# The products with V of a pair of heads in one run of four key tiles, in a differential attention and mixture-of-experts kernel

## The reference

```
Q, K: [8 batches, 16 heads, 512, 128]      V: [8, 16, 512, 64]
Q1, Q2 = Q[..., :64], Q[..., 64:]          K1, K2 likewise
A1 = Q1 @ K1.T / 8                         A2 = Q2 @ K2.T / 8
P = softmax(A1) - lam * softmax(A2)        [.., 512 queries, 512 keys]
O = P @ V                                  the products that the change moves
Y = concat_heads(O) @ Wo + bo, then a layer norm, times 0.2
```

## Time and profile before

| | before |
|---|---|
| median of 3 runs | 2054.06 us (2049.75 to 2055.78) |
| the profiled execution, its own time | 2053.49 us |
| its span in the trace | 2051.5 us |
| PE busy, share of the span | 93% |
| DVE, ACT, POOL busy | 78%, 73%, 44% |
| mean granted TensorE clock | 0.98 of full speed |

### The profile page before, as it was taken

One profiled execution on the slowest core, in us unless ns is written; L12 is line 12 of the kernel. 1 busy time (PEld: TensorE's weight loads), 2 busy tenths in 40 slices (PEclk: granted clock), 3 DMA queues, 4 the chain that ended last, 5 costly groups with the idle time before them and its releaser, 6 DMA issues. The chain is left out here.

```text
span 2051.5 us, 39312 instructions
## 1 busy us (share of the span) xinstructions
PE 1903.1 (93%) x10625; PEld 1465.2 (71%) x10625; DVE 1609.2 (78%) x2960; ACT 1493.6 (73%) x3383; POOL 909.5 (44%) x893
## 2 busy tenths in 40 slices
PE   4369999999999999999999999999998699997885
PEld 4347767776777677767767776777675699997885
DVE  5448888888888888888888888888887456664566
ACT  3348888888888888888888888888887466665332
POOL 1234444444444444444444444444433365564676
PEclk9999999999999999999999999999999899999888
DMA  5778888788778777887888787777873866672564
GB/s 174 275 226 215 210 210 215 197 210 213 209 200 212 211 206 204 212 215 198 208 211 215 198 209 212 216 195 209 211 191 78 317 222 235 244 223 98 169 213 125
DMA packets 162207, 421.05 MB, mean 205 GB/s; under 512 B 27794, under 2 KB 69568, under 8 KB 146944
## 3 DMA queue, kind: packets, MB, share of 16 engines
q1 hardware_dynamic: 157408, 410.42, 70.7%
q0 software_dynamic: 4768, 10.25, 1.8%
HBM read 177.53 MB, written 41.72 MB: 107 GB/s over the span
## 5 line engine op out<-in xcount | busy, mean ns | idle before, releaser
L567 POOL TENSOR_TENSOR e<-e,rrec 128x512 f32<-128x512 f32 x512 | 532.1, 1039 | 832.1 <-DVE rrec L683 832.1
L644 ACT ACTIVATE e<-p_score,nmax 128x512 f32<-128x512 f32 x1024 | 695.2, 684 | 136.3 <-DVE nmax L708 135.5
L708 DVE TENSOR_REDUCE nmax<-p_score 128x2 f32<-128x1024 f32 x512 | 626.8, 1224 | 152.8 <-PE p_score L766 148.4
L766 PE MATMUL p_score<-ks,qs 128*128 128x512 f32 x2048 | 575.0, 402 | 6.6 <-ACT e L644 3.8
L754 PE MATMUL p_proj<-xp,w 128*128 (+1 forms) x1920 | 524.6, 409 | 21.2 <-SPq L482 21.2
L766 PEld LDWEIGHTS p_score<-ks,qs 128*128 128x128 f32 x2048 | 369.6, 188 | 180.6 <-ACT e L644 53.9
L754 PEld LDWEIGHTS p_proj<-xp,w 128*128 128x128 f32 x1920 | 339.8, 190 | 80.4 <-SPq L482 21.9
L694 DVE SCALAR_TENSOR_TENSOR pm<-e,coef 128x512 f32<-128x512 f32 x512 | 388.9, 760 | 0.0
L611 ACT COPY pT<-p_tr 128x512 f32<-128x512 f32 x512 | 301.3, 588 | 98.4 <-PE p_tr L776 97.8
L776 PE MATMUL p_tr<-consts,pm 128*128 128x128 f32 x2048 | 307.2, 273 | 2.3 <-ACT pT L611 2.3
L776 PEld LDWEIGHTS p_tr<-consts,pm 128*128 128x128 f32 x2048 | 254.6, 140 | 71.2 <-issue 2.5
(11 more groups left out here) (137 smaller groups left out, 1735.1 us busy)
## 6 DMA issues: line engine op xcount, KB each, us to landing
ks<-k_parts SPq DMA_DIRECT2D x512, 256.0 KB, 4.3
w<-weight_parts_scratch SPq DMA_DIRECT2D x64, 1280.0 KB, 8.1
qs<-q_parts SPq DMA_DIRECT2D x512, 128.0 KB, 2.9
w<-in_w SPq DMA_DIRECT2D x46, 1024.0 KB, 7.7
oT_scratch<-oT SPq DMA_DIRECT2D x64, 256.0 KB, 4.7
oTs<-oT_scratch SPq DMA_DIRECT2D x16, 1024.0 KB, 16.5
ys_scratch<-y SPq DMA_DIRECT2D x23, 256.0 KB
weight_parts_scratch<-n_wt_parts SPq DMA_DIRECT2D x4, 1280.0 KB, 7.3
```

The source lines that it names most:

```text
L567: nc.gpsimd.tensor_tensor(e1, e1, rrec[:, t % 4, 0:1].to_broadcast([P, S]), ALU.mult).then_inc(s_e1, 1)
L644: nc.scalar.activation(ex[:, t % 4, m, :], p_score[t % 2][:, m, :], ACT.Exp, bias=nmax[:, t % 2, m:m + 1], accum_out=rsum[:, t % 4, m:m + ...
L708: nc.vector.tensor_reduce(nmax[:, t % 2, :], p_score[t % 2][:, :, :], AXX, ALU.max, negate=True).then_inc(s_max, 1)
L766: last_op = nc.tensor.matmul(p_score[st % 2][:, m, :], qs[j][u][:, m, qt * P:(qt + 1) * P], ks[j][u][:, m, part, :], start=(part == 0), st ...
```

## The change

The table that says in which step which key tiles are multiplied has one entry in place of three. The two matmuls of each key tile, their operands, their order among themselves and the waits ahead of the first of them (`s_pT`, `s_v`, `s_o`) stay as they are.

```
@@ -459,7 +459,7 @@
         ORDER = ("q0", "k0", "q1", "k1", "v", "vt")
         AT_STEP = {0: "q0", 1: "k0", 2: "q1", 3: "k1", 4: "v", 6: "vt"}
 
-        PV_STEP = {5: (0,), 6: (1,), 7: (2, 3)}
+        PV_STEP = {5: (0, 1, 2, 3)}
 
         def batch_of(pair):
             return pair // PAIRS
```

## The result

| | before | changed |
|---|---|---|
| median | 2054.31 us (4 runs) | 2068.48 us (2067.58 to 2070.21, 4 runs) |
| ratio to before | | 1.0074, 95% interval 1.0056 to 1.0091 |
| the profiled execution, its own time | 2053.49 us | 2067.92 us |
| its span | 2051.5 us | 2066.0 us |

A forecast was written before the change was run, and what follows sets the result against it. The prediction took PE to set the pace, with the other engines following. It summed 2053.5 + 11.2 (62 pairs at 0.18) + 1.5 (last pair and tail) = 2066.2, put at 2066 us; 2055 to 2079 held 8 in 10.

The forecast's parts named there:

- The wait in step 0: PE waits 0.54 us before the next pair's step 0 scores for step 6's exponentials; pair 0.18 us longer; chance 0.69.
- The entries: Two entries into the products vanish per pair, at 0.17 to 0.20 us each; 0.36 us saved.
- the rival without a wait: Step 0's scores find their buffer free at 8.72 us, so the saving stands: 2031 us, chance 0.07.
- The case without a difference: PE's wait before step 0's scores takes 0.36 us and eats just the saving: 2053 to 2058 us, chance 0.12.
- The copy of V: DVE's copy before projection k0 in step 1 keeps 0.27 us margin; rival: it becomes a second wait, 2079 us, chance 0.10.
- No debt into the next pair: From step 2 PE is slowest again; by the next step 5 all engines are back at their earlier distance.
- The clock: Expected to stay at 1.00 through the attention; rival: PE's wait lowers it, near 2230 us, chance 0.02.
- The sum: Pairs 1 to 62 add 62 x 0.18 = 11.2 us, last pair and tail 1.5 us, stages behind untouched: 2066.2 us.

The follow-up runs named there:

- short maxima: Row maxima taken over 128 of the 512 keys: in the changed kernel 2044.10 us (0.9950), in the kernel before 2049.74 us (0.9977).
- doubled transposes: Three of the four transposes of step 7 done twice: in the kernel before 2074.65 us (1.0108), in the changed kernel 2068.60 us (1.0074).
- run in step 6: All four key tiles multiplied in step 6 in place of step 5, all else as in the changed kernel: 2065.49 us, ratio 1.0047.

## Why the prediction was right

**The wait in step 0.** Right in its place, its cause and its end. Forecast were 5.26 us to the scores of step 6, a chain of 3.94 + 0.06 and 9.26 us to the scores of step 0; measured were 5.25, 3.94 + 0.05 and 9.24. The short maxima show that this chain sets the time, and the doubled transposes show that PE has slack there and only after the change. How long PE waits was not right: 0.8 us and not 0.54, by the next term. The idle of 0.56 us in PE's row agrees with the forecast by luck, since that row hides a part of the wait.

**The entries.** The one term of the pair that was mis-sized. I put two entries at 0.36 us, read as the idle ahead of the products. They cost 0.62 (22.69 - 22.38 = 0.31 for one, taken twice), since leaving them costs as well. PE alone would have been at the scores of step 0 at 8.46 and not at 8.72, and so waits 0.8 us and not 0.54. This changed nothing in the result, because the end of a wait doesn't depend on when it begins. For the rival without a wait it did: its time would have been 2053.5 - 62 x 0.62 = 2015, not 2031, and the run or the chain would have had to be 0.8 us shorter for it, not 0.54.

**The case without a difference** was drawn at the right distance. The wait would have had to end 0.19 us earlier, against 0.18 in the forecast, and it hung on the size of a tile, which was read right: runs of one to four tiles take 1.01, 1.87, 2.72 and 3.59 us, 0.85 to 0.87 for each further tile.

**The copy of V.** Right: forecast from 12.41 to 13.10 us with 0.27 us to spare, measured from 12.46 to 13.14 with 0.22. The run in step 6 has it 0.3 us too late, and there PE does wait for it. But not everything beyond the margin is added, as the forecast had it: without that wait the pair is 0.13 us shorter, and not 0.3, since another wait takes its place.

**No debt into the next pair.** Right: steps 1 to 4 are as before, within 0.01 us.

**The clock.** Right: 1.00 from 400 to 800 us. By this trace TensorE stays at its level of 2.4 GHz with a wait of 0.8 us in each pair; steps 6 and 7 took 1.80 and, without the wait, 1.37 us. The Trainium skill (TensorE: Matmul & The Clock Gate, Part 4: PE-mode transpose) says that transposes don't count toward a busy TensorE as other matmuls do. Among scores and projections, this trace shows no fall of the clock by them.

**The sum.** Pairs 1 to 62 took 11.7 us more, against 11.2 forecast. The last pair and the tail took 2.3 us more, against 1.5: its scores of step 6 came 2.65 us later (15.99 against 13.34 from the start of the pair), and the rounds of the tail took up only 0.3 of that. The rest of the 14.5 us of span lies outside what the change touches: the attention began 1.2 us later, pair 0 took 1.4 us more (granted clock 0.92 from 131 to 153 us, in the profile before 1.00 there), and the stages behind the attention gave 2.1 us back. That these three nearly cancel is luck. No products are taken in pair 0, and its 19.0 us in the kernel before are 20.2 and 20.5 in two other kernels with the table of before (short maxima and doubled transposes).

The windows of that stretch in the changed kernel:

```profile
131.00:153.00 22.00, 19.02 (x82) 14.78 (x82) 16.78 (x30) 14.54 (x37) 8.23 (x9) 0.92 0.96 259
```

## What to carry to other kernels

With two buffers between engines, any two steps in a row must last as long as the chain that frees a buffer (here 4.0 us from scores to the end of their exponentials, and more where DVE or ACT comes late to it, as with the run in step 6), so work that is gathered in one step is missing as cover in the next: look at the pair of steps that gets short, not at the one that gets long. Gathering does save the way in and out of a group, here 0.31 to 0.36 us each, and the best tables of this study save one of the two and leave the cover: three tiles in step 5 and one in step 7, at 2035 us, or two and two, at 2037, which these runs don't tell apart. Where a wait ends by another engine's chain, an error in what lies before the wait doesn't reach the result, but it does reach every comparison with a kernel that has no such wait.

## What was not expected of the hardware

A group of products with 64 weight columns among groups with 128 costs 0.31 to 0.36 us beyond its matmuls (0.86 us a key tile), about 0.19 ahead of it and 0.15 behind it, whether transposes of V, scores or a projection follow. In every kernel here the transposes of `pm` stand ahead of it, and no run shows whether the 64 columns are the cause. The page of the profile shows nothing of it in PE's busy time, which stood at 400 of 400 us in the kernel before; only PEld's idle (0.17 us ahead, 0.81 behind) and the distances between starts do.
